# The order of two pieces of TensorE work inside one step of a software pipeline: the use of a shared PSUM bank first, the products with the values second

## The kernel before: how a sixteen-head stage is staged

| step | use of the shared bank | who reads it out, and when |
|---|---|---|
| g0 l0, g0 l2 | q, k projection (L801) | DVE `rotate` (L1064) in l2a and l3a; ACT (L870) and DVE (L1073) in l2b; ACT (L866) in l0b; same step |
| g0 l1, g0 l4 | rotated copies of q and k (l2a, l3a; L801) | DVE `rotate` (L1064), steps l1 and l5 |
| every group, l3 | back: transposes of `oT` (L815), the last group's result | DVE `weighted` (L1080 to L1088), step l4 |
| g0 l5 | attnT: transposes of the whole output (L818; not l0b) | ACT into `aoT` (L901), g1 l0 |
| g1 l1 | output projection (L821; not l0b) | DVE `add_output` (L1110, in l2b L1114), g1 l2 |
| g1 l2, g3 l1 | max: transposes of the split maxima (L810) | ACT into `mT` (L907), behind the exponentials of steps g1 l3 and g3 l2; SP then places it with two DMAs |
| g1 l4 | v projection (L805) | DVE (L1179) or ACT (L918, L914), g1 l5 |

## Time and profile before

### The profile page before, as it was taken

The page is one execution under the profiler, slowest core; times in us unless marked ns, Lnnn a source line. Parts: engine busy times, 40 slices in busy tenths (PEclk is TensorE's granted clock), DMA queues, the critical chain, the costliest instruction groups (busy, mean ns, idle before and its releaser), DMA issues. The chain is left out here.

```text
span 3871.3 us, 64184 instructions
## 1 busy us (share of the span) xinstructions
PE 2797.9 (72%) x22261; PEld 1744.1 (45%) x22261; DVE 2614.4 (68%) x5832; ACT 1779.5 (46%) x3174; POOL 1620.8 (42%) x2248
## 2 busy tenths in 40 slices
PE   5869367776595668678588867687756788677946
PEld 4769212221595347557333335333334333354535
DVE  4645578886555863363388849688858788586768
ACT  2423246666321324344246653366643466645633
POOL 7655522220445223233356640256631466503743
PEclk9879679999697769879789989599978799897977
DMA  7123232220232012102122200122100222000000
GB/s 194 46 71 98 53 99 89 77 73 2 91 91 67 1 51 72 28 8 72 55 82 77 82 2 1 67 84 78 41 1 8 93 76 76 18 1 1 1 3 20
DMA packets 220978, 207.97 MB, mean 54 GB/s; under 512 B 49672, under 2 KB 197832, under 8 KB 219897
## 3 DMA queue, kind: packets, MB, share of 16 engines
q1 hardware_dynamic: 208376, 178.69, 14.3%
q0 software_dynamic: 12288, 25.19, 2.1%
HBM read 103.94 MB, written 97.91 MB: 52 GB/s over the span
## 5 line engine op out<-in xcount | busy, mean ns | idle before, releaser
L1036 DVE TENSOR_REDUCE l0b_negm<-l0b_ps_s 128x2 f32<-128x1024 f32 x256 | 304.2, 1220 | 55.4 <-PE l0b_ps_s L760 54.4
L850 ACT ACTIVATE l0b_E<-l0b_ps_t 128x1024 f32<-128x1024 f32 x242 | 247.8, 1024 | 124.2 <-PE l0b_ps_t L742 124.1
L1036 DVE TENSOR_REDUCE l2b_negm<-l2b_ps_s 128x2 f32<-128x256 f32 (+3 forms) x256 | 197.0, 819 | 30.9 <-PE l2b_ps_s L765 30.7
L850 ACT ACTIVATE l2a_E<-l2a_ps_t 128x768 f32<-128x768 f32 (+1 forms) x182 | 160.3, 881 | 118.2 <-PE l2a_ps_t L742 117.4
L850 ACT ACTIVATE l3a_E<-l3a_ps_t 128x768 f32<-128x768 f32 (+1 forms) x182 | 160.3, 881 | 117.1 <-PE l3a_ps_t L742 116.3
L1036 DVE TENSOR_REDUCE l3a_negm<-l3a_ps_s 128x2 f32<-128x256 f32 (+3 forms) x256 | 196.7, 818 | 17.2 <-PE l3a_ps_s L765 17.0
L1036 DVE TENSOR_REDUCE l2a_negm<-l2a_ps_s 128x2 f32<-128x256 f32 (+3 forms) x256 | 196.5, 817 | 15.6 <-PE l2a_ps_s L765 15.5
L850 ACT ACTIVATE l2b_E<-l2b_ps_t 128x768 f32<-128x768 f32 (+1 forms) x182 | 160.2, 880 | 99.2 <-PE l2b_ps_t L742 98.3
L937 POOL TENSOR_SCALAR_AFFINE_SELECT l2b_E<-l2b_E 128x256 f32<-128x256 f32 x256 | 99.8, 406 | 140.9 <-ACT l2b_E L850 140.0
L937 POOL TENSOR_SCALAR_AFFINE_SELECT l2a_E<-l2a_E 128x256 f32<-128x256 f32 x256 | 100.7, 407 | 135.8 <-ACT l2a_E L850 133.5
L937 POOL TENSOR_SCALAR_AFFINE_SELECT l3a_E<-l3a_E 128x256 f32<-128x256 f32 x256 | 100.7, 407 | 134.0 <-ACT l3a_E L850 131.7
(11 more groups left out here) (1016 smaller groups left out, 8545.8 us busy)
## 6 DMA issues: line engine op xcount, KB each, us to landing
room_up<-l0b_stack SPq DMA_DIRECT2D x32, 192.0 KB
room_down<-l0b_stack SPq DMA_DIRECT2D x32, 192.0 KB
room_up<-l2a_stack SPq DMA_DIRECT2D x32, 192.0 KB
room_down<-l2a_stack SPq DMA_DIRECT2D x32, 192.0 KB
room_up<-l2b_stack SPq DMA_DIRECT2D x32, 192.0 KB
room_down<-l2b_stack SPq DMA_DIRECT2D x32, 192.0 KB
room_up<-l3a_stack SPq DMA_DIRECT2D x32, 192.0 KB
room_down<-l3a_stack SPq DMA_DIRECT2D x32, 192.0 KB
```

The source lines that it names most:

```text
L850: act.activation(probs(n % 3, c, 0)[:, 2 * p:2 * p + 2, :], scores_room(T)[:, :, 0:width[c]], ACT.Exp, scale=scale).then_inc(probs_ready.s ...
L1036: e = dve.tensor_reduce(negm[:, qt, :, j], ps_s[n % 2][:, :, off:off + keys[qt]], AX.X, ALU.max, negate=True)
```

## The change

In a step that has both, PE now issues the use of the shared bank ahead of the products with the values. Nothing else is moved: the loops of ACT, DVE, POOL and SP, and every semaphore and count, stay as they are. In even steps, which have no products, nothing changes.

```
                 if T % 2 == 0 and 0 <= T + 3 * L < ALL:
                     scores(T + 3 * L)
                     scores(T + 3 * L + 1)
+                for what, n in spare_uses(b, g, l):
+                    spare(what, n)
                 if T % 2 == 1 and 0 <= T - 3 < ALL:
                     values((T - 3) // 2)
-                for what, n in spare_uses(b, g, l):
-                    spare(what, n)
```

## The result

The changed kernel takes 3936.9 us (median of 4 executions, 3936.1 to 3938.9), the kernel before 3864.0 us (median of 4, the one execution more taken beside the changed kernel). The ratio is 1.0193, 95% interval 1.0181 to 1.0206: slower by 1.9%, some 74 us, where 55 were forecast (the quotient of the two medians, 1.0189 or 73 us, lies inside the interval). In what follows a ratio is turned into us with 3862, the median of the first three executions before.

What follows compares the result with a forecast made beforehand. PE and ACT alternating on score banks set the pace in steps without other work, PE's own work in fuller steps. 34.2 + 5.4 + 2.2 + 13.0 = 54.8, say 55, on the median 3861.9: 3917 us, range 3880 to 3948.

Steps and rivals of the forecast that it cites:

- step l3 of group 1: Every batch of four stages: transposes can't start earlier, products follow uncovered, 32 x 1.07 = 34.2 us lost.
- group 0, all three terms: Lost cover in group 0, batches 1 to 5: 5.4 us in l2b, 2.2 in l0b, 13.0 in the rotary stages.
- step l1 of groups 1 and 3, step l3 of groups 2 and 3: Small loss from later products set against small gain from earlier transposes: 0, ends -10 and +18 us.
- clock rival: PE's new idling in step l3 of group 1 also lowers its clock: 32 us added, cost 87, 3949 us; chance 0.18.
- rotary stages: Group 0, batches 1 to 5: PE loses 2.09 per batch, DVE's wait absorbs part; 6.5 us per stage, 13.0 in all.
- the 5.4: l2b, step l3 of group 0, batches 1 to 5: products added whole behind the transposes, 5 x 1.07 us.
- 2.2: l0b, step l3 of group 0, batches 1 to 5: PE idles 0.45 for ACT's reading, 5 x 0.45 us.
- The small gain at step l4: Group 2: DVE gets transposes earlier, but its next maxima need later scores; at most 0.3 us per batch gained.
- the loss that I had bounded by 18: Step l3 of group 3: PE waits for the maxima's copy, at most 0.57 us per batch, +18 over 32.
- DVE absorbs the lot: DVE's waits take most of the lost time: within 0.3%, some 12 us; chance 0.07, shared with nothing changed.
- Faster: Step l4: DVE's maxima follow the earlier transposes at once, gaining 24 to 32 us, about 3835 us; chance 0.05.
- Nothing changes: PE lets ready products pass the waiting use, so the time stays; chance 0.07, shared with all absorbed.

Runs made afterwards that it cites:

- the first experiment: Kernel before with the shared-bank use ahead of the products only in step l3 of group 1, old order elsewhere: ratio 1.0155, 60 us slower.

## Why the prediction came out as it did

The sign and the mechanism held, and the time lies inside the range; the likeliest value was 20 us too low, and two misses of opposite sign, in step l3 of group 1 and in group 0, cancel in part. That l2a and l3a grew by 14.1 and 16.5 us where 15 was forecast for each is luck of this kind. Every step of the sum against what was measured:

| step | predicted, us | measured, us |
|---|---|---|
| step l3 of group 1 | 34.2 | 50 in the full change (74.5 - 24.3), 60 alone; 28 and 29 with the idle time filled |
| group 0, all three terms | 20.6 | 14 alone |
| step l1 of groups 1 and 3, step l3 of groups 2 and 3 | 0 (-10 to +18) | 7 for three of these four steps |
| all but step l3 of group 1 | 20.6 | 24 |
| sum | 55 | 74 |

**The step that was mis-sized is "step l3 of group 1".** Its mechanism is right: PE's wait ahead of L815 became 1.37 us (1.59 in l0b) in seven batches of eight and 1.71 (1.85) in the last, 46.8 us in all, where 1.45 and 1.66 were written down, and the products moved behind. With the idle time filled, this order costs 28 us in one experiment, and 53 - 24 = 29 in the other, a little under the 34.2. What the term left out is the clock: 50 - 29 = 21 us in the changed kernel. The traces show both parts by the batch. In batches 1 to 6 of l2a and l3a the changed kernel takes 0.88 to 1.00 us longer than the kernel with all but this step where the clock holds, so 28 to 32 for all 32 places, and 2.34 to 2.56 longer in the six where a stretch at 1.2 GHz begins at the place. The changed kernel has 13 such places, the kernel with all but this step none; at some 1.5 us each that is 20 us, as much as the filling gave back. The prediction had found the clock low in twelve batches (in one of them, batch 4 of l2a, a wait of 0.11 was left, so the cover wasn't whole), kept 1.07 for all, and priced the clock only as a rival in which all twenty others get a slow stretch; of these, ten did.

**The clock rival was therefore partly true,** as an addition to my forecast, not in its place. The measured cost lies above 70, where the prediction had its rival with 0.18 and its own forecast ended; as two outcomes with chances that exclude each other, it had no case for "both, in part". The sign that it named for the rival, PEclk well below 0.95, did not show (0.94 to 0.96): the other steps of the change run with less time at 1.2 GHz (82 us with all but this step, 124.5 and 110 before), and the average hides what this step adds. The reason that I gave against the rival, that the wait for DVE ahead of the place shrinks, holds: at the eight places behind the 1.56 us (batches 2 to 5 of l2a and l3a) the clock was low at 6 in the kernel before (7 in its second profile), at 7 with step l3 of group 1 alone, and at 2 in the changed kernel, where the wait is 0.27.

**Group 0** was priced too high in the rotary stages, at 13.0. In the run with group 0 alone PE comes to the wait in step l2 of group 1 later by 1.69, not 2.09, and the wait shrinks from 1.56 to 0.44:

```profile
2190.42 0.34 PE L760 MATMUL l2a_ps_s<-room_down,room_up 48*128 48x384 bf16 x2 [0.44 <-DVE l2a_negm L1041]
```

In this batch (5 of l2a, which had kept its clock before) 0.56 us of delay is left where 1.1 stood. And with the wait the low clock went too, from 6 of the eight places named above to none: those six batches are even 0.2 to 0.5 us shorter than before. So in the profiles the two stages last as long as before (0.3 us more and 0.1 less). In l2b the 5.4 came as written, 5.7 us of waits in 5 batches, and in l0b 1.8 where 2.2 stood.

**The steps set to 0** cost 7 us for three of the four. The small gain at step l4 was spent again: DVE's next maxima wait for scores, which was the argument; the loss that I had bounded by 18 is there in part.

**The other rivals fell.** *DVE absorbs the lot*: the stages grew by 62.7 us, and PE's waits for the maxima (L760) fell by only 16 us over the four stages, from 78.0 to 61.6. *Faster*: DVE did get the transposes earlier, 49.6 us less waiting, and waited 110.9 us more for scores; and the three uses that wait for little, moved alone, cost 7 us. *Nothing changes*: PE stood 1.37 us in front of the waiting transposes with the products ready behind them, and no product ran ahead. The rule of the Trainium skill that the prediction named there (TensorE: Matmul & The Clock Gate, section Step-by-step: what each phase is for), matmuls in program order, agrees with the 32 waits of this trace.

What stays open: how much of the 24 us of the other steps is clock and how much cover. The kernels that contain only these steps show less time at 1.2 GHz than the kernel before (82 us with all but step l3 of group 1, against 110 and 124.5), so their cover may cost somewhat more than the medians say. Outside group 0 it was not taken apart.

## What to carry to other kernels

On an engine that works in order, put ready work ahead of the instruction that has to wait, and look for what the waiting instruction waits for: here a copy that stood behind an exponential on ACT for no need, and with the copy moved the new order costs 15 us where it cost 74 (23 against the old order with the same copy, which gains 8.5). When a change makes PE idle in a place that repeats, price the clock with it, as part of the forecast and not only as a rival, and look at the idle times just ahead of that place as well. A filler of redundant matmuls in the idle time shows the two apart: it leaves the order and the waits of the other engines, and here it gave back 1.5 us in the batches whose clock had fallen and nothing in the others.

## What the runs showed of the hardware

- More matmuls made a kernel faster: 34 us of redundant products took the first experiment's kernel from 1.0155 to 1.0073, and the changed kernel from 1.0193 to 1.0137.
- Idle times of 1.37 to 1.71 us were followed by the 1.2 GHz level in some batches and not in others. In the changed kernel a stretch at that level begins at 13 of the 32 places, with the idle time filled at none, and each cost about 1.5 us where single batches can be compared. The idle time alone does not decide it: the same wait with the same busy time ahead of it (2.06 and 2.05 of 3.90 us) kept PEclk at 1.00 in one place and brought 0.50 in another.
- The clock of one program differs between its executions: 124.5 and 110 us at 1.2 GHz in the sixteen-head stages of the kernel before, most of the difference in l0b, whose length was 421.3 and 412.5 us.
